# Two attention-then-MLP layers on one core: three positions in the hand-written step plan are changed

## The chip, the core and the metric

One core of a Trainium2 chip runs the whole program, built in Bass with every wait written by hand. The metric is device time in microseconds. The kernel before takes 3954.84 us, the median of three runs (3951.35 to 3958.53).

Five engines work side by side, each through its own queue of instructions in program order: TensorE (PE, matmuls into PSUM), VectorE (DVE), ScalarE (ACT), GpSimd (POOL), and SyncE (SP), which here only issues DMAs. An instruction that waits for a semaphore holds back all that stands behind it on its engine.

## What is computed

Input x is 4 sequences of 1024 tokens with 512 channels. Two transformer layers follow each other, each with 16 heads of width 32 and an MLP of width 2048. Cut to what matters:

```python
# layer 0
h = ada_norm(x, cond); q, k, v = h @ wq + bq, h @ wk + bk, h @ wv + bv
q, k = rotary(q), rotary(k)
x = x + softmax(q k^T / sqrt(32)) v @ wo + bo
x = x + gelu(ada_norm(x, cond) @ w1 + b1) @ w2 + b2
# layer 1: 4 key/value heads shared by 16 query heads, gates from the condition
h = ln(x) * (1 + sc1) + sh1
x = x + g1 * (softmax(q k^T / sqrt(32)) v @ wo.T)
x = x + g2 * (gelu((ln(x) * (1 + sc2) + sh2) @ w1.T + b1) @ w2.T + b2)
```

Products are made of two float16 halves of each operand (three matmuls for one), except values and totals, which are float32.

## The kernel before

The work is eight passes `i` = 0 to 7: layer 0 for the four sequences, then layer 1. Each pass is an attention and a forward part (the MLP). Both are written out by steps, and each engine's program walks the same steps.

**The attention** has 64 steps (`STEPS`), eight for each of eight blocks (4 heads by 512 queries). Step `s` computes four score tiles of 128 keys by 512 queries, `w` = 4s to 4s+3; two tiles make a unit `u`, so units 2s and 2s+1. Scores use three PSUM banks. ACT takes the exponential of each tile into `probs`, which has room for six units (L1209). PE multiplies the units of two steps before with the values (`values`, L1029). For the softmax's denominators POOL adds the probabilities of units u-2 and u into `sums`, which has three slots (`add_probs`, L730): sum 2p and 2p+1 need the units of step 2p+1. The last eight sums (56 to 63) of a pass are added by DVE (L1525). Then `totals` (L1044) multiplies the pair of sums 2p and 2p+1 with ones, on PE. `totals_step` says in which step PE does that for pair p; it stands at the end of the step, after the values.

Three waits tie these together. ACT writes unit u only when the sum that holds unit u-6 is done (L1204): units 4p+6 and 4p+8 wait for sum 2p, units 4p+7 and 4p+9 for sum 2p+1. The add of sum m waits for the totals of pair (m-3)//2 (L727, L1524). Totals wait for both sums of their pair (L1035).

**Beside it** PE computes the raw scores of the following block (`max_in_columns`, mostly four tiles per step, none in steps 56 to 63), and DVE takes each row's maximum (L1532); in the steps with s % 8 == 6, `max_rows` brings the maxima of a block together (DVE `mfin` L1537, a transpose on PE L977, `mT` on DVE L1541). These tiles, and all "fills", go through three more PSUM banks in turn. Fills are other products put between the scores of chosen steps (`fills_of`): projections of queries, keys and values; from step `WO_AT` the output products of the first half of the tokens, one per step (`out_tile`, keys `wo`), each read by DVE's `residual` (L1496 to L1505); in steps `LN2_AT` and `LN2_AT`+1 the second norm's chunks, two per step (`norm_chunk` on PE L852 and ACT L1167, `norm_lo` on DVE L1453, L1454). After the fourth output product DVE gathers the statistics (L1418, L1420), POOL computes the deviation (L708, L710) and DVE applies it (`norm_apply`, L1430) in its program order in that same step. DVE adds its sums at the end of a step, in steps 57 to 63 (`vector_step`).

**In layer 0** POOL also turns the queries and keys (`turns`: L715, L716, L720, L721) and adds a bias to eight tiles of x (L738, at the sums named in `BIAS_AT`, 49 to 56). In passes 0 to 3 ACT and DVE also split weights into halves for later (`SPLITS`: ACT L1235, DVE `split_low` L1582): each split takes two steps of DVE, from step 3 on in every third step, 18 splits in pass 0 and seven in passes 1 to 3. After each block ACT copies the outputs (L1215) and totals (L1221), POOL multiplies with the inverse (L762), and both finish the block (ACT L1191, in layer 0 also L1195; POOL L768), in fixed places: the values' copy in step 1 of the next block, the totals' copy in step 3, the finish of the block before that at the end of step 2.

**The forward part** has 33 steps of PE-heavy products. Its first product needs the second norm's chunks, and stands behind the last totals in PE's order.

Of the kernel before, what the change touches and what calls it, by code (L numbers as in the profile page):

```python
# [38 lines left out]
L0_CHUNKS, L1_CHUNKS = 24, 21  # L39
MAX_AT = (4, 6, 8, 10, 12, 14, 16, 18, 20, 22, 24, 26, 28, 30, 32)  # L40
MAX_AT_K = (0, 2, 5, 7, 9, 11, 14, 16, 18, 20, 23, 25, 27, 29, 32)
WO_AT = 53
LN2_AT = 60
BIAS_AT = (49, 49, 50, 51, 53, 54, 56, 56)
TURNS = ((("k", 1, 0), -1, 1, 5), (("k", 1, 1), 3, 3, 10), (("q", 0, 1), 11, 13, 29), (("q", 1, 1), 25, 27, 57))

# [1 line left out]
def layer(i):  # L48
    return i // B
# [30 lines left out]
def totals_step(i, pair):  # L80

    if pair >= SUMS // 2 - 2:
        return STEPS - 1 if pair == SUMS // 2 - 2 else STEPS + 1
    return 2 * pair + (3 if layer(i) == 0 and pair < 2 else 4)


def by_vector(m):
# [11 lines left out]
def fills_of(i):  # L99
# [12 lines left out]
    for t in range(4):  # L112
        at[WO_AT + t] = [("wo", i, t)]
    for t in range(2):
        at[LN2_AT + t] = [("ln2", i, 0, 2 * t), ("ln2", i, 0, 2 * t + 1)]
    return at
# [166 lines left out]
def program(nc, ins, out):  # L283
    ctx = ExitStack()
    with ctx:
# [546 lines left out]
        def _(pe):  # L832
# [215 lines left out]
            def attention(i):  # L1048
                for s in range(STEPS + LAG // 2):
                    u = 2 * s  # L1050
                    if s < STEPS:
                        maxima, fills = maxima_at(i, s), FILLS[i].get(s, [])
                        max_in_columns(maxima[0:1])
                        score(i, 4 * s)
                        max_in_columns(maxima[1:2])
                        score(i, 4 * s + 1)
                        for key in fills:
                            fill(key, 0, 6 if key[0] in "kqv" else 12)
                        max_in_columns(() if fills else maxima[2:3])
                        score(i, 4 * s + 2)  # L1060
                        for key in fills:
                            if key[0] in "kqv":
                                fill(key, 6, 12)
                        max_in_columns(maxima[2:3] if fills else maxima[3:4])
                        score(i, 4 * s + 3)
                        max_in_columns(maxima[3:] if fills else maxima[4:])
                    if LAG <= u < UNITS + LAG:
                        values(i, u - LAG)
                    for pair in range(SUMS // 2):
                        if s == totals_step(i, pair):  # L1070
                            totals(i, 2 * pair)
                    some(rows_at(i, s))
# [725 lines left out]
```

## Time and profile before

| | us |
|---|---|
| median of three runs | 3954.84 |
| lowest, highest | 3951.35, 3958.53 |
| the profiled execution, its time | 3957.61 |
| its span, first to last instruction | 3955.8 |
| busy: PE, DVE, POOL, ACT | 3746.3, 2471.2, 1613.5, 1603.8 |
| mean granted TensorE clock | 0.98 |

The rows below are of that one execution. Line numbers (L931) are those of the kernel before. A row of a timeline has the start, the duration, the engine, line and operation, what it writes and reads, how many instructions it joins, and, in brackets, how long the engine was idle before and what ended that. A matmul's duration is longer than its share of the engine, since matmuls overlap; what a group costs is read from one start to the next.

### The profile page before, as it was taken

To read this page: it belongs to the slowest core of one execution; us is meant where nothing else is said; L and a number is where in the kernel's file an instruction comes from. 1 tells how busy PE (TensorE), PEld (TensorE's weight loads), DVE (VectorE), ACT (ScalarE), POOL (GpSimd) and SP (SyncE) were. 2 spreads that over 40 slices of the span, in tenths; PEclk is the share of its full clock that TensorE was granted. 3 is DMA by queue.
4 is the path that set the end of the run, shared out by engine and by line. 5 is a ranking of instruction groups with operands and counts; after the bars stand their busy time and mean duration, and the time that the engine had idled before them with its cause. 6 is when DMAs were issued, how large, how long until landed. Compare 5 with 4: busy or idle time off the path is not lost.

```text
span 3955.8 us, 76367 instructions
## 1 busy us (share of the span) xinstructions
PE 3746.3 (95%) x31828; PEld 1559.4 (39%) x31828; DVE 2471.2 (62%) x3951; ACT 1603.8 (41%) x2807; POOL 1613.5 (41%) x907
## 2 busy tenths in 40 slices
PE   7988999999998989999899999999999999999999
PEld 4422444333543335433354333433344333543344
DVE  5677735766457755467654777467664776467752
ACT  1466313554125642155521663136621563126621
POOL 2467212672216742066510672137520672126611
PEclk8899999999999999999999999999999999999999
DMA  5233243212423123431232112311123112311122
GB/s 153 48 99 119 85 107 81 72 55 84 109 76 87 41 91 91 106 75 53 100 101 83 34 42 89 115 44 29 65 96 98 31 40 81 114 54 26 63 67 96
DMA packets 139110, 306.67 MB, mean 78 GB/s; under 512 B 19680, under 2 KB 59636, under 8 KB 137872
## 3 DMA queue, kind: packets, MB, share of 16 engines
q10 hardware_dynamic: 50944, 174.62, 13.6%
q1 hardware_dynamic: 87824, 127.17, 12.1%
q8 instruction: 253, 4.15, 0.4%
q14 instruction: 89, 0.73, 0.1%
HBM read 223.46 MB, written 36.66 MB: 66 GB/s over the span
## 4 chain that ended last, share of the span: by engine, by line
PE 79%; DVE 7%; POOL 5%; issue 4%; ACT 3%; DMA 1%; ACTq 0%; SPq 0%; POOLq 0%; DVEq 0%
PE ps L931 15%; PE ps L834 12%; PE ps L835 12%; PE ps L836 12%; PE ps L1029 9%; PE ps L871 7%; PE ps L1044 5%; PE ps L888 3%; POOL sums L730 3%; ACT probs L1209 3%; DVE mcol L1532 2%; PE ps L947 2%; PE ps L852 1%; DVE ring L1582 1%; DVE turn L1466 1%
## 5 line engine op out<-in xcount | busy, mean ns | idle before, releaser
L1532 DVE TENSOR_REDUCE mcol<-ps 128x1 f32<-128x512 f32 x2048 | 1290.0, 683 | 441.2 <-PE ps L931 226.7
L730 POOL TENSOR_TENSOR sums<-probs 128x1024 f32<-128x1024 f32 x448 | 1065.2, 2392 | 943.0 <-PE ps L1044 510.9
L1209 ACT ACTIVATE probs<-ps 128x512 f32<-128x512 f32 x2048 | 1098.8, 608 | 812.0 <-PE ps L931 564.3
L931 PE MATMUL ps<-qs,ks 98*32 98x512 f16 x8192 | 800.6, 389 | 105.4 <-ACT probs L1209 93.5
L931 PE MATMUL ps<-ks,qs 97*32 97x512 f16 x7040 | 697.3, 385 | 53.7 <-DVE mcol L1532 41.5
L1355 ACT ACTIVATE sums<-ps,cols 128x512 f32<-128x512 f32 x256 | 175.8, 687 | 1097.0 <-PE ps L836 1097.0
L1029 PE MATMUL ps<-probs,v_sb 128*32 128x512 f32 x4096 | 548.5, 612 | 0.0
L931 PEld LDWEIGHTS ps<-qs,ks 98*32 98x32 f16 x8192 | 215.5, 97 | 589.9 <-ACT probs L1209 363.9
L834 PE MATMUL ps<-ring,probs 128*128 128x512 f16 x1024 | 388.0, 379 | 0.3 <-DVE probs L1627 0.3
L834 PE MATMUL ps<-aT,ring 128*128 128x512 f16 x1024 | 388.1, 379 | 0.0
L836 PE MATMUL ps<-aT,ring 128*128 128x512 f16 x1024 | 388.0, 379 | 0.0
L835 PE MATMUL ps<-aT,ring 128*128 128x512 f16 x1024 | 387.9, 379 | 0.0
L836 PE MATMUL ps<-ring,probs 128*128 128x512 f16 x1024 | 387.9, 379 | 0.0
L835 PE MATMUL ps<-ring,probs 128*128 128x512 f16 x1024 | 387.8, 379 | 0.0
L931 PEld LDWEIGHTS ps<-ks,qs 97*32 97x32 f16 x7040 | 188.4, 96 | 375.8 <-DVE mcol L1532 150.5
L1626 DVE CAST probs<-sums 128x512 f16<-128x512 f32 x256 | 132.7, 518 | 320.2 <-ACT sums L1355 320.2
L871 PE MATMUL ps<-hT,wqkv 128*128 128x512 f16 x1248 | 302.7, 388 | 8.8 <-DVE hT L1454 7.5
L1044 PE MATMUL ps<-sums,ones 128*32 128x512 f32 x2048 | 276.2, 615 | 1.0 <-DVE sums L1525 1.0
L715 POOL TENSOR_TENSOR turn<-turn 128x512 f32<-128x512 f32 x32 | 44.9, 1403 | 532.5 <-DVE turn L1466 532.5
L1627 DVE TENSOR_TENSOR probs<-sums,probs 128x512 f16<-128x512 f32 x256 | 203.7, 796 | 8.8
L1466 DVE SCALAR_TENSOR_TENSOR turn<-ps,bias,trig 128x512 f32<-128x512 f32 x128 | 90.2, 747 | 167.1 <-PE ps L871 167.1
L871 PEld LDWEIGHTS ps<-hT,wqkv 128*128 128x128 f16 x1248 | 115.9, 99 | 172.6 <-issue 33.5
(112 smaller groups left out, 3471.9 us busy)
## 6 DMA issues: line engine op xcount, KB each, us to landing
ring<-halves ACTq DMA_DIRECT2D x208, 512.0 KB, 3.3
qs<-hl SPq DMA_DIRECT2D x192, 128.0 KB, 4.1
ring<-halves SPq DMA_DIRECT2D x48, 512.0 KB, 6.2
ring<-in_weights ACTq DMA_DIRECT2D x39, 512.0 KB, 4.6
halves<-ring ACTq DMA_DIRECT2D x37, 512.0 KB, 2.9
ks<-hl SPq DMA_DIRECT2D x120, 128.0 KB, 4.4
dcopy<-inverses SPq DMA_DIRECT2D x56, 256.0 KB
probs<-in_x SPq DMA_DIRECT2D x8, 1024.0 KB, 8.3
```

Source lines behind the costliest of these rows:

```text
L730: pool.tensor_tensor(sums[:, m % SUM_SLOTS, :, :], prob(u - 2), prob(u), ALU.add).then_inc(sum_set[0].sem, 1)
L834: pe.matmul(dst, lhs[0], rhs[0], start=first, stop=False)
L835: pe.matmul(dst, lhs[0], rhs[1], start=False, stop=False)
L836: return pe.matmul(dst, lhs[1], rhs[0], start=False, stop=last)
L871: mm = pe.matmul(bank, qkv(lw, weight_at(kind, i, hh, part, c), P), hT[:, lx, c, tok], start=(q == 0), stop=(q == 11))
L931: mm = pe.matmul(bank[cut, :], lhs[:, cut], rhs, start=True, stop=True)
L1029: mm = pe.matmul(ps[32 * q:32 * q + 32, 4, :], values_of(i, hh)[:, kt, value_cut(i, hh, 4 * g + q)], prob(u + q // 2)[:, q % 2, :], start= ...
L1044: mm = pe.matmul(ps[32 * q:32 * q + 32, 5, :], ones32[:, :], sums[:, (m + q // 2) % SUM_SLOTS, q % 2, :], start=(m % 8 == 0), stop=(m % 8 ...
L1209: act.activation(prob(u)[:, e, :], ps[:, w % SCORE_BANKS, :], ACT.Exp).then_inc(exp_done.sem, 1)
L1355: act.activation(g32[:, n % 2, :], ps[:, 4 + n % 2, :], ACT.Gelu, bias=col[:, n % FC:n % FC + 1], scale=1 / WS).then_inc(gelu_done.sem, 1)
L1532: dve.tensor_reduce(mcol[:, blk % 2, 4 * j + qt, half:half + 1], src, AX.X, ALU.max).then_inc(n_free[0], 1)
L1627: dve.tensor_tensor(fT[:, n % 4, 1, :], g32[:, n % 2, :], fT[:, n % 4, 0, :], ALU.subtract).then_inc(f_set.sem, 1)
```

## The change

`totals_step` gives step 2p+3 for every pair but the last two. Before, it gave 2p+4, except for the first two pairs in layer 0. `WO_AT` goes from 53 to 55: the output products of the first half of tokens are in steps 55 to 58. `LN2_AT` goes from 60 to 62: the second norm's chunks are in steps 62 and 63. `norm_apply` follows the fourth output product, so it moves to step 58 too. `BIAS_AT`, `vector_step`, and the places of all other work stay.

```diff
-WO_AT = 53
-LN2_AT = 60
+WO_AT = 55
+LN2_AT = 62
...
     if pair >= SUMS // 2 - 2:
         return STEPS - 1 if pair == SUMS // 2 - 2 else STEPS + 1
-    return 2 * pair + (3 if layer(i) == 0 and pair < 2 else 4)
+    return 2 * pair + 3
```

## Rows read from the trace of the kernel before

**Rows 1.** The page, part 1: busy us, share of the span, instructions.
```profile
PE 3746.3 (95%) x31828; PEld 1559.4 (39%) x31828; DVE 2471.2 (62%) x3951; ACT 1603.8 (41%) x2807; POOL 1613.5 (41%) x907
```

**Rows 2.** Waits: engine, line, waited for: us in total, times, longest.
```profile
PE ps L931 <- ACT probs L1209: 93.5, 135, 3.4
...
ACT probs L1209 <- POOL sums L730: 113.8, 84, 3.2
...
POOL sums L730 <- PE ps L1044: 510.9, 189, 8.9
```

**Rows 3.** Stretches: length, busy us of each engine, granted clock, DMA share, GB/s.
```profile
3138.84:3165.02 26.18, 25.64 (x357) 8.91 (x353) 20.78 (x35) 18.09 (x35) 21.17 (x10) 1.00 0.20 42
1235.62:1283.65 48.03, 39.54 (x490) 12.48 (x486) 40.51 (x59) 29.50 (x52) 37.91 (x18) 0.93 0.30 84
241.59:367.52 125.93, 108.23 (x1311) 35.49 (x1307) 103.16 (x150) 80.90 (x143) 85.27 (x42) 0.94 0.32 105
1283.65:1395.23 111.58, 108.03 (x1351) 38.98 (x1347) 79.46 (x133) 70.69 (x133) 80.32 (x43) 0.98 0.19 54
1395.23:1451.90 56.67, 47.05 (x433) 16.25 (x425) 30.62 (x44) 28.67 (x53) 25.85 (x17) 0.94 0.18 66
...
3262.43:3295.09 32.66, 28.74 (x249) 9.60 (x245) 18.51 (x32) 14.01 (x26) 15.34 (x9) 0.95 0.28 106
...
3295.09:3317.71 22.62, 19.04 (x188) 6.15 (x180) 14.63 (x16) 14.07 (x26) 1.60 (x1) 0.92 0.04 13
```

**Rows 4.** Timeline of PE, attention 6, steps 18 and 19.
```profile
3143.59 0.40 PE L931 MATMUL ps<-qs,ks 98*32 98x512 f16 x4 [0.36 <-ACT probs L1209]
...
3144.68 1.03 PE L1044 MATMUL ps<-sums,ones 128*32 128x512 f32 x8
3145.53 0.39 PE L931 MATMUL ps<-ks,qs 97*32 97x512 f16 x4
...
3148.14 0.39 PE L931 MATMUL ps<-ks,qs 97*32 97x512 f16 x4
```

**Rows 5.** Timelines of POOL and of ACT, attention 6, step 23.
```profile
3158.74 4.70 POOL L730 TENSOR_TENSOR sums<-probs 128x1024 f32<-128x1024 f32 x2 [1.70 <-PE ps L1044]
...
3161.23 2.06 ACT L1209 ACTIVATE probs<-ps 128x512 f32<-128x512 f32 x4 [0.78 <-POOL sums L730]
```

**Rows 6.** Timelines of DVE and of PE, attention 6, step 22.
```profile
3157.53 0.19 DVE L1537 TENSOR_REDUCE mfin<-mcol 128x16 f32<-128x32 f32 x1
...
3158.48 0.28 PE L977 MATMUL ps<-ident,mfin 128*16 128x128 f32 x1
```

**Rows 7.** Timeline of ACT, attention 2, end of step 34.
```profile
1327.07 0.77 ACT L1191 ACTIVATE aT<-ocopy,cols 128x512 f16<-128x512 f32 x1
```

**Rows 8.** Timeline of ACT, attention 2, end of step 17.
```profile
1255.35 1.08 ACT L1209 ACTIVATE probs<-ps 128x512 f32<-128x512 f32 x2 [2.92 <-POOL sums L730]
```

**Rows 9.** Timelines of DVE and of PE, attention 2, step 22.
```profile
1271.03 2.79 DVE L1582 SCALAR_TENSOR_TENSOR ring<-ring 128x512 f16<-128x512 f32 x1
...
1274.47 0.62 PE L931 MATMUL ps<-ks,qs 97*32 97x512 f16 x4 [1.88 <-DVE mcol L1532]
```

**Rows 10.** Timeline of PE, attention 6, step 55: first and last of twelve.
```profile
3277.11 0.39 PE L834 MATMUL ps<-wo,aT 128*128 128x512 f16 x1
...
3279.50 0.38 PE L836 MATMUL ps<-wo,aT 128*128 128x512 f16 x1
```

**Rows 11.** Timelines of POOL and of DVE, attention 2, step 58.
```profile
1423.19 1.02 POOL L710 TENSOR_TENSOR rs<-sd,eps 128x4 f32<-128x4 f32 x1
...
1424.25 2.77 DVE L1430 TENSOR_SCALAR v_sb<-ks,mv,rs 128x512 f32<-128x512 f32 x4 [6.63 <-POOL rs L710]
```

**Rows 12.** Timeline of DVE, attention 6, step 62.
```profile
3306.87 0.81 DVE L1453 TENSOR_SCALAR turn<-ps,ab 128x512 f32<-128x512 f32 x1 [1.49 <-ACT aT L1167]
...
3309.77 1.22 DVE L1525 TENSOR_TENSOR sums<-probs 128x1024 f32<-128x1024 f32 x1
```

**Rows 13.** Timeline of POOL, attention 2, step 51.
```profile
1391.28 2.52 POOL L738 TENSOR_TENSOR ks<-ks,row_bc 128x512 f32<-128x512 f32 x2
```

## The prediction

> **What bounds the kernel now.** I read first the page's busy times: TensorE (PE) works 3746.3 of 3955.8 us [rows 1]. So what can be won is the 209 us in which it stands, less the start, unless work is taken away, and this change takes none away. Second, the waits [rows 2]: PE waits 93.5 us for ACT's exponentials, ACT in turn 113.8 us in 84 places for POOL's sums, and POOL waits 510.9 us for PE's totals (L1044). That is a ring: totals release a slot of `sums`, POOL adds into it, the finished add releases a slot of `probs`, ACT writes it, PE may issue the next score. Third, stretches by stage [rows 3]: eight steps without fills in the second layer's blocks take 26.18 us; the layer 0 stretch of steps 13 to 23 takes 48.03 us at PE 39.54 busy; the last steps (from 53 to the first forward product) take 56.67 us in layer 0 and 32.66 + 22.62 = 55.28 in layer 1. Fourth, the timeline of single steps.
>
> A step without fills, in the shortest form that the trace has, runs from its first maximum to that of the next step in 2.61 us (3145.53 to 3148.14 [rows 4]). Totals add 0.86, from their start at 3144.68 to that maximum at 3145.53 [rows 4]: 3.47 us at best. The trace's even steps, which hold totals now, are longer than that. Attention 6, steps 16 to 23: 3.47, 2.61, 4.31, 2.61, 3.81, 2.61, 4.13, 2.61, the 26.18 of the stretch. In each odd step the third exponential waits for an add that could start only after the totals at the end of the step before: POOL starts two adds back to back, having waited 1.70 us for the totals [rows 5], and the exponential at 3161.23 waits 0.78 for the first of them [rows 5]. PE pays in the following even step: the score at 3143.59 waits 0.36 beyond its cadence [rows 4].
>
> **Part 1: totals in step 2p+3.** 30 of 32 pairs per attention move, save two in layer 0 that are there already and the last two. No instruction is added. The same 0.86 us of PE goes from an even to an odd step. The odd add of each pair waits for the pair before, now done one step earlier, so it starts as soon as its exponential is there: the adds (2.37 each [rows 5]) end well before the next odd step. Of eight steps: four odd ones at 3.47, three even at 2.61, and one with the rows of maxima. There the transpose (L977) follows the totals today, at 3158.48 [rows 6]. Without the totals in that step PE reaches it 0.86 earlier and waits until DVE's `mfin` is there (3157.53 + 0.19, in a step that now begins later by the stall above): it saves 0.6 of the 0.86, and that step takes 3.5. Sum 13.9 + 7.8 + 3.5 = 25.25, 0.93 less than 26.18. This is the cover that goes: totals hid a wait of DVE of about 0.6.
>
> A second cover goes. In every eight steps ACT ends step 2 with the finish of a block, two activations in layer 0 (0.77 us the first [rows 7], 1.4 for both). The totals hide that today. In a step of 2.61 the next exponential comes about 0.75 late and the fourth score with it, about 0.55: layer 0 gains 0.4 per eight steps, not 0.93. In layer 1 the single activation fits.
>
> Layer 1, steps 8 to 52: 5.6 times 0.93 = 5.2. Against it: step 14, where a fill's `hl` and two maxima follow the fill on DVE until `mfin`; that chain, not the totals, sets its end, so the moved 0.86 is simply added in step 13: minus 0.9. Steps 26 and 27 lose 0.6 in the same way (an estimate, from maxima 0.6 apart behind a fill). At the start POOL's first adds stand in line with four output sums, so totals in steps 3 and 5 wait for them on PE: minus 0.6. Net 3.1; ends 0 and 6.
>
> Layer 0, steps 13 to 23: here stalls are large. The exponential at 1255.35 waits 2.92 us for a sum [rows 8], and three before it 0.3 to 2.0, since POOL, with rotation and stack lows between its adds, starts each late. With one step more of slack these four go. And DVE's split (L1582) takes 2.79 us at 1271.03, where it starts 0.1 after an add and ends when that is over, and under 0.7 with POOL idle; PE then waits 1.88 for a maximum [rows 9]. **The rule**: the Trainium skill, SBUF — State Buffer, section "Who interferes with whom", says that a DVE instruction with two SBUF inputs and a GpSimd instruction that reads SBUF exclude each other for the whole of the one that came first. Here the row agrees. By that rule the change would move the blocks, not end them: see the third rival. From the rows: now adds start with the step in which the split is queued, so a blocked split waits for a whole add (2.1). After it, an add of an odd step starts at about 1.6 and ends at 4.0, the split comes at 2.6, so it waits 1.4; in an even step it waits 0.3. Stalls of PE in these eleven steps, counted as length less the cadence of every matmul group, are 14.8 us now; by the timeline drawn again with the same durations 8.5: 6 saved, ends 1 and 10.
>
> Layer 0, steps 24 to 52: POOL's second turning (steps 25 to 30) stalls 2.8 now and 0.6 then, minus 0.8 at step 26, plus 2.6 times 0.4: 2.4. In attention 0 these steps take 125.93 us against 111.58 in attention 2 [rows 3]; the difference is 22 more split halves and their blocks. By the same 1.4 and 0.3 half of them stay: another 5, ends 0 and 12. Steps 0 to 12: 0.5.
>
> **Part 2: output products at 55 to 58, second norm at 62 and 63.** A product is 12 matmuls, 3277.11 to 3279.50 and one more, 2.6 us [rows 10]. Of four, two leave steps 53 and 54, where DVE must also take maxima. They go to 57 and 58, which have neither fills nor maxima. Redrawn: steps 53 to 58 of layer 1 take 3.5, 3.35, 5.4, 4.5, 5.4, 4.5 = 26.7, with the same four products and three totals for which they take 32.66 now [rows 3]. What is late next is DVE's order. After the fourth product DVE does `ks`, stats and aggregates (1.9), POOL the deviation (1.3, of it L710 1.02), DVE four applications (2.77 [rows 11]; 1.9 with POOL idle) and only then the add of sum 57 (1.22 [rows 12]). Today that falls in step 56 and has two steps of room. At step 58 the add ends some 6.1 us into step 59 (5.3 in layer 0, which has one operation less per product). The exponential of unit 119 and the totals of pair 28 want it at 1.5 and 1.7: 4.4 us of stall, 3.6 in layer 0. Today steps 58 and 59 stall too, 4.3 in layer 1 and 6.7 in layer 0. At the end, chunks 3 and 4 now lie in front of the adds 62 and 63: from the add of 61, exponential, activation, two chunks of the norm (3306.87 to 3309.77, 2.9 [rows 12]), two adds and the totals in line make 0.6 + 0.8 + 2.9 + 2.5 + 1.0 = 7.8 us. Before them, from the start of step 62 to the end of the add of 61: 2.3 to the exponential behind the chunks' transposes, 1.4 to DVE, 2.9 for two chunks, 1.3: 7.9. Laid end to end, step 59 takes 7.2, 60 takes 2.2, 61 takes 2.9 and the rest 15.7: 28.0 us in layer 1, for 22.62 now [rows 3], and 27.1 in layer 0. Whole stretch: layer 1 54.7 against 55.28, 0.6 saved; layer 0 53.8. To that come 1.2, as POOL's bias additions (1.26 each [rows 13], with adds between them) make sum 51 late for totals now in step 53: 55.0 against 56.67, 1.7 saved. Ends for either: 4 lost, 6 saved. Nothing of this passes SP's or ACT's DMA queues: loads keep their places, and the reload of x, issued in step 49, had landed when these biases ran at 1391.28, two steps later [rows 13].
>
> **Sum.** Layer 1: 3.1 + 0.6 = 3.7, four times 15. Layer 0, attentions 1 to 3: 0.5 + 6 + 2.4 + 1.7 = 10.6, three times 32. Attention 0: 10.6 + 5 = 15.6, taken as 13, since its splits run on into steps 54 and 55. Together 60 us. The profiled execution took 3957.61 us with a span of 3955.8; the median shown is 3954.84. Profiled: 3957.6 - 60 = 3897.6; median 3954.8 - 60 = 3895.
>
> **Rivals.**
> 1. The mechanism holds as drawn: 3895. Chance 0.57.
> 2. PE waits for POOL. Totals a step earlier are in PE's program order, so whenever POOL is late the whole engine stands, where before only ACT did. For it: layer 0's rows of POOL, which is 37.91 of 48.03 us busy [rows 3]. Against it: an add ends 1.5 steps before its totals in the plain step. If it eats layer 0's gain but for the end, 15 + 7 remain: 3933. Chance 0.12.
> 3. The lock between DVE and POOL. If each of some 37 split halves in odd steps meets an add at its start (2.1 instead of 1.4, and 1.5 of it reaches PE), 0.7 to 1 more is lost for each: 30 us back, 3925. The same chance speaks for less: some pairs miss each other. This is what the Trainium skill's page SBUF — State Buffer would lead one to expect. Chance 0.13.
> 4. No change: the stalls of steps 58 to 63 double as the clock falls behind them (0.94 granted there, 1.00 in the plain steps [rows 3]), and the rest of the gain is eaten by them; 3950. The stalls are there today, so this needs 6 more per attention than drawn. Chance 0.08.
> 5. Slower: the end of attention. Add 57 behind the norm on DVE is a serial chain of five operations over two engines. Each of them late costs PE directly, and so do the adds 62 and 63 behind four chunks. If the two cost 4.4 + 8 us on top, not in place, of what stalls there now (12.4 in each of 8 attentions, 99 us) less 75 gained elsewhere, it is 24 slower: 3979. It decides from 7.5 us per attention on. Against it: today's stalls of 12 to 15 us in these steps have the same cause and go with it. Chance 0.10.
>
> Faster: 0.57 + 0.12 + 0.13 = 0.82; same 0.08; slower 0.10. 0.2%, 7.9 us, is about what a measurement of this kernel can tell from no change. Range: above, rivals 2 and 3 and the lower ends of layer 1 (0) and of the splits, 3938; below, the upper ends, some 30 us more, 3865.
>
> **What would show it.** ACT's wait for POOL's sums falls from 113.8 to under 40 us; POOL's wait for totals falls and its wait for ACT grows. Eight plain steps take 25.3 us, and L977 begins to wait for `mfin`, 0.5 each time. Split halves of 2.7 us become rare and halves of 2 common. A new wait of some 4 us stands in step 59, of PE for ACT and of ACT for DVE's sums. The prediction is wrong if PE waits for POOL's sums at L1044 for more than some 20 us in all, or if the last stretch is longer than 57 us.

## The result, and the profile after

The kernel after takes 3928.73 us (median; 3922.8 to 3928.93). Beside it, on the same chip, the kernel before took 3955.41 (3951.35 to 3958.53). The ratio is 0.993, with a 95% interval of 0.9912 to 0.9947: 26.7 us or 0.7% faster. Forecast were 3895 and a gain of 60. The direction and the range held, the size was over twice too large.

The page of the kernel after, span and busy times (us, share of the span, instructions), against [rows 1]:

```profile
span 3927.1 us, 76367 instructions
...
PE 3707.2 (94%) x31828; PEld 1609.8 (41%) x31828; DVE 2447.3 (62%) x3951; ACT 1609.2 (41%) x2807; POOL 1608.9 (41%) x907
```

The same 31828 matmuls take 39 us less of busy time, but the span is only 28.7 shorter. The waits of the kernel after (engine, what it works on, what it waited for: us in total, times, longest), against [rows 2]:

```profile
PE ps L1044 <- DVE sums L1525: 57.7, 24, 4.2
PE ps L977 <- DVE mfin L1537: 32.8, 54, 1.4
PE ps L931 <- ACT probs L1209: 20.8, 35, 1.3
...
PE ps L1044 <- POOL sums L730: 7.0, 9, 0.9
...
ACT probs L1209 <- DVE sums L1525: 48.5, 16, 4.5
ACT probs L1209 <- POOL sums L730: 18.1, 13, 2.0
...
POOL sums L730 <- PE ps L1044: 86.8, 46, 5.4
```

The old ring is open: ACT waits 18.1 us for POOL's sums (113.8 in [rows 2]), POOL 86.8 for totals (510.9), PE 20.8 for exponentials (93.5). At the top is a new wait: PE stands 57.7 us, in 24 places (three per attention), before totals whose sums **DVE** adds. These are the last sums of each attention.

I laid the step starts of the two traces beside each other. All eight attentions summed, in us:

| steps | after less before | forecast |
|---|---|---|
| 0 to 7 | +6.5 | |
| 8 to 12 | -14.3 | |
| 13 to 23 | -15.0 | |
| 24 to 52 | -30.1 | |
| 0 to 52 together | -52.9 | -50.4 |
| 53 to 58 | -27.0 | |
| 59 to 62 | -12.6 | |
| 63 to the first forward product | +57.9 | |
| 53 to the end together | +18.3 | -9.2 |
| forward parts (seven between attentions) | +5.7 | 0 |

The table tells of the two profiled executions, and that its row of steps 0 to 52 comes so near the forecast is in part luck (see below). Up to step 52 the sum is within 2.5 us of the forecast. Steps 53 to 62 gain 39.6, and the last stretch loses 57.9. That is where the expected gain went. The stretches that answer to [rows 3], of the kernel after (length, busy us of PE, PEld, DVE, ACT, POOL, granted clock, DMA share, GB/s): the plain eight steps of attention 6; steps 13 to 23 and 24 to 52 of attention 2; 24 to 52 of attention 0; then in attention 6 steps 53 to 58, 59 to 62, and from 63 on:

```profile
3110.99:3136.28 25.29, 24.78 (x357) 10.59 (x353) 20.63 (x35) 18.22 (x35) 21.28 (x11) 1.00 0.20 44
...
1218.12:1261.33 43.21, 36.46 (x499) 12.89 (x491) 38.99 (x61) 29.54 (x52) 33.45 (x17) 1.00 0.33 93
1261.33:1371.62 110.29, 106.98 (x1340) 42.75 (x1343) 77.72 (x131) 70.91 (x133) 82.58 (x43) 0.97 0.19 55
237.60:358.21 120.61, 103.12 (x1299) 36.19 (x1303) 105.08 (x149) 81.11 (x143) 90.69 (x45) 0.95 0.33 107
...
3233.58:3260.27 26.69, 26.18 (x251) 9.45 (x246) 15.37 (x24) 13.18 (x25) 11.39 (x6) 1.00 0.35 129
3260.27:3277.87 17.60, 12.60 (x124) 4.04 (x120) 9.26 (x16) 9.45 (x19) 3.62 (x4) 0.81 0.05 17
3277.87:3291.29 13.42, 8.08 (x68) 2.19 (x61) 9.23 (x11) 5.58 (x10) 0.00 (x0) 0.91 0.04 8
```

The plain block was forecast at 25.25 and takes 25.29. Steps 53 to 58 were forecast at 26.7 and take 26.69. The last two rows together are 31.02 us, for a forecast of 28.0, with PE standing over 10 of them.

**Step 59** of attention 6 in the kernel after. DVE's timeline, then POOL's, then PE's:

```profile
3263.09 2.74 DVE L1430 TENSOR_SCALAR v_sb<-ks,mv,rs 128x512 f32<-128x512 f32 x4 [1.41 <-POOL rs L710]
3265.76 2.35 DVE L1525 TENSOR_TENSOR sums<-probs 128x1024 f32<-128x1024 f32 x2
```
```profile
3262.04 1.02 POOL L710 TENSOR_TENSOR rs<-sd,eps 128x4 f32<-128x4 f32 x1
3263.03 1.15 POOL L768 TENSOR_TENSOR aT<-ocopy,aT 128x512 f16<-128x512 f32 x1
```
```profile
3267.07 1.94 PE L1044 MATMUL ps<-sums,ones 128*32 128x512 f32 x8 [4.16 <-DVE sums L1525]
```

DVE waits 1.41 us for the deviation, applies the norm in 2.74, and only then adds sums 57 and 58. PE waits 4.16 for the first of them. This is the stall that the forecast drew. Two of its sizes are not as drawn. The four applications take 2.74 and not 1.9, since POOL's finish of a block starts at 3263.03, 0.06 before them. And the eight matmuls of the totals take 1.94 us, where they take 1.03 in [rows 4].

### The profile page after: what moved, and what is told of

The parts are those of the page before. It is cut to its first block, busy times and chain, and to the rows that moved or that the text cites. A ratio compares the mean times of both kernels' runs of the same rounds, so it can differ in the third digit from the quotient of the medians.

```text
span 3927.1 us, 76367 instructions
## 1 busy us (share of the span) xinstructions
PE 3707.2 (94%) x31828; PEld 1609.8 (41%) x31828; DVE 2447.3 (62%) x3951; ACT 1609.2 (41%) x2807; POOL 1608.9 (41%) x907
## 4 chain that ended last, share of the span: by engine, by line
PE 80%; DVE 12%; issue 3%; POOL 2%; ACT 1%; DMA 1%; ACTq 0%; SPq 0%; POOLq 0%; DVEq 0%
PE ps L931 16%; PE ps L834 13%; PE ps L835 12%; PE ps L836 12%; PE ps L1029 8%; PE ps L871 7%; DVE mcol L1532 6%; PE ps L1044 5%; PE ps L888 3%; PE ps L947 2%; DVE ring L1582 1%; PE ps L852 1%; DVE sums L1525 1%; POOL sums L730 1%; ACT probs L1209 1%
## 5 line engine op out<-in xcount | busy, mean ns | idle before, releaser
L931 PE MATMUL ps<-qs,ks 98*32 98x512 f16 x8192 | 801.6, 388 | 26.6 <-ACT probs L1209 20.8
L931 PE MATMUL ps<-ks,qs 97*32 97x512 f16 x7040 | 708.2, 385 | 45.0 <-DVE mcol L1532 31.8
L931 PEld LDWEIGHTS ps<-qs,ks 98*32 98x32 f16 x8192 | 227.7, 98 | 357.5 <-ACT probs L1209 151.9
L931 PEld LDWEIGHTS ps<-ks,qs 97*32 97x32 f16 x7040 | 197.3, 96 | 407.1 <-DVE mcol L1532 206.5
L1044 PE MATMUL ps<-sums,ones 128*32 128x512 f32 x2048 | 280.1, 621 | 64.7 <-DVE sums L1525 57.7
```

The costliest lines, as they stand in the source:

```text
L931: mm = pe.matmul(bank[cut, :], lhs[:, cut], rhs, start=True, stop=True)
L1044: mm = pe.matmul(ps[32 * q:32 * q + 32, 5, :], ones32[:, :], sums[:, (m + q // 2) % SUM_SLOTS, q % 2, :], start=(m % 8 == 0), stop=(m % 8 ...
```

## The experiments

Each is compared with the kernel before on the same chip, whose medians lie from 3952.13 to 3957.19. "Tail" is step 53 to the first forward product, all eight attentions summed, less that of before. My theory: the two parts of the change (part 1, the totals' step; part 2, the places of products and chunks) are a gain and a cost, and the cost sits in DVE's order at the end of each attention.

### One part at a time

**Totals alone**, the kernel after with the other two positions as before:

```diff
-WO_AT = 55
-LN2_AT = 62
+WO_AT = 53
+LN2_AT = 60
```

> Totals in step 2p+3 as in the changed kernel, products and norm chunks left at 53 and 60. Theory A (the missing gain is in the last eleven steps, because the late products put DVE's norm in front of the add of sum 57): steps 0 to 52 keep their gain of some 53 us and the last stretch does not grow from 56 to 58 us per pass; total near 3900, at least 20 us under the changed kernel's 3928.7. Theory B (the two parts need each other: with products in steps 53 and 54 the totals of step 53 and the maxima stall, and moving them is what keeps the gain): 3930 or more.

Measured: 3869.02 us (3865.64 to 3873.46), ratio 0.9791 [0.9776, 0.9806]. That is 83 us off the kernel before, against 27 for the whole change, and below what either theory had said. Tail -27.6. Its waits, then from attention 6 its stretches of steps 53 to 58, 59 to 62, and from 63 on:

```profile
PE ps L931 <- ACT probs L1209: 41.4, 59, 1.7
...
PE ps L1044 <- DVE sums L1525: 9.7, 15, 0.9
```
```profile
3184.91:3215.49 30.58, 28.15 (x249) 9.74 (x245) 16.85 (x34) 13.01 (x25) 12.55 (x8) 0.94 0.30 113
3215.49:3230.99 15.50, 11.84 (x132) 4.49 (x128) 10.31 (x13) 11.89 (x23) 1.81 (x1) 1.00 0.05 18
3230.99:3238.37 7.38, 5.67 (x60) 1.50 (x53) 6.01 (x5) 3.09 (x6) 1.46 (x1) 1.00 0.02 6
```

PE's wait for DVE's sums is 9.7 us in place of 57.7. The tail of before was long because its totals were late, and earlier totals alone shorten it.

**Products and second norm alone**, the kernel before with `WO_AT = 55`, `LN2_AT = 62`:

> Products at 55 to 58 and chunks at 62 and 63, totals left as in the kernel before. Theory A: this part alone costs, some 2 to 4 us per pass in the last stretch: 3970 to 3985. Theory B: steps 53 and 54 lose their stall of some 2 to 3 us per pass and nothing comes in its place: 3930 to 3940.

Measured: 3975.42 us, ratio 1.0057 [1.004, 1.0074]: 23 us slower. Tail +11.9, forward parts +8.3. So part 1 alone brings 83 us, part 2 alone costs 23, and both bring 27: on top of part 1, part 2 costs 56. In the tail part 2 costs 11.9 us on top of the kernel before and 46.0 on top of part 1. The profiled executions of the kernel after and of totals alone lie 60 apart, 7.5 per attention. Of the 60, 46.0 are in the tail, 5.7 in the forward parts, and 7.5 in steps 0 to 52, most of it in attention 0 (last section).

**Products late, norm chunks early** (the kernel after with `LN2_AT = 60`):

> The changed kernel with the norm's chunks back in steps 60 and 61; the products stay late at 55 to 58. Theory A (each of the two moves costs by itself, in its own place): the stall of some 4 us at the totals of step 59 stays, the wait of the last totals behind two chunks and two adds goes; the last stretch is some 55 to 56 us instead of 57.8, total 3910 to 3920. Rival (the chunks do all the harm): some 52 us, total 3870 to 3880.

Measured: 3903.51 us, ratio 0.988 [0.9861, 0.9899]; tail +3.0, forward parts 0. That is a tail of 56 us per attention, as expected; the time is 6 us under the expected range.

**Products early, norm chunks late** (the kernel after with `WO_AT = 53`):

> The changed kernel with the products back at 53 to 56; the norm's chunks stay late in 62 and 63. Theory A: no stall at the totals of step 59, but from step 63 to the first forward product 13.4 us instead of 7.4, of which steps 60 and 61 give back 3 to 4; last stretch 54 to 56, total 3895 to 3915. Rival (the products do all the harm): 52 us, total 3870 to 3880.

Measured: 3894.15 us, ratio 0.985 [0.9833, 0.9867]; tail -17.1, forward parts +8.8. That is a tail of 53.5 us per attention, and it and the time are just under the expected ranges. Each half of part 2 costs by itself: in the tail, against -27.6, the products' move 30.6 and the norm's 10.5. Steps 59 to 62 of attention 6, and what follows, first products late with norm early, then the other way round:

```profile
3235.21:3256.63 21.42, 13.68 (x133) 5.14 (x128) 13.40 (x23) 11.93 (x23) 2.35 (x3) 0.92 0.04 13
3256.63:3264.01 7.38, 5.66 (x61) 1.50 (x54) 6.01 (x5) 3.09 (x6) 1.38 (x1) 1.00 0.02 7
```
```profile
3239.76:3251.25 11.49, 10.30 (x124) 3.63 (x120) 6.03 (x6) 9.44 (x19) 2.76 (x2) 1.00 0.08 26
3251.25:3263.81 12.56, 7.21 (x69) 2.15 (x61) 9.24 (x11) 5.57 (x10) 0.32 (x1) 1.00 0.01 2
```

The two costs have two places. With products late, PE stands in steps 59 to 62 (21.42 us at PE 13.68 busy). With chunks late, it stands from step 63 on (12.56 at 7.21).

### Only DVE's order changed

**Add 57 in front of the norm**, all positions as in the kernel after:

```diff
-                        if key == ("wo", i, 3):
-                            norm_apply("ln2", i, 0)
...
                             add_probs(i, m)
+                    if s == WO_AT + 3:
+                        norm_apply("ln2", i, 0)
```

> The changed kernel with one thing moved on DVE: in step 58 the add of sum 57 stands ahead of the four applications of the second norm, not behind them. Theory A: the stall of 4.2 us of PE at the totals of step 59 goes, step 59 falls from 8.5 to 4 us or less, eight passes give 30 to 40 us, 3890 to 3900. Rival: the applications, now 1.2 us later, or the clock, set the end all the same, 3920 to 3930.

Measured: 3894.4 us, ratio 0.9855 [0.984, 0.987]: 58 us off the kernel before, where the whole change takes off 27, with the same instructions. DVE's timeline of step 59 in attention 6, then the stretches of steps 59 to 62 and from 63 on:

```profile
3230.32 1.18 DVE L1525 TENSOR_TENSOR sums<-probs 128x1024 f32<-128x1024 f32 x1
...
3232.69 2.75 DVE L1430 TENSOR_SCALAR v_sb<-ks,mv,rs 128x512 f32<-128x512 f32 x4 [1.20 <-POOL rs L710]
```
```profile
3228.98:3242.15 13.17, 10.49 (x126) 3.70 (x121) 8.99 (x16) 9.56 (x19) 3.24 (x3) 1.00 0.06 19
3242.15:3255.84 13.69, 8.44 (x68) 2.71 (x61) 10.35 (x11) 5.56 (x10) 1.27 (x1) 0.87 0.02 6
```

The add no longer stands behind DVE's wait for POOL. Steps 59 to 62 fall from 17.60 to 13.17, all at the full clock, and the end stays as long. Against the kernel after, the tail is 29.3 us shorter; another 8.4 come in steps 0 to 52, most of them in attention 0, where no order was changed (last section).

**Adds 61 and 62 in front of the chunks too:**

```diff
                         max_item(key)
+                    if s >= 62:
+                        add_probs(i, s - 1)
...
-                        if by_vector(m) and vector_step(m) == s:
+                        if by_vector(m) and vector_step(m) == s and m not in (61, 62):
```

> As add57_first, and in steps 62 and 63 DVE adds sums 61 and 62 before the norm's chunks of the same step. Theory A: besides the stall of step 59, the exponential of unit 127 no longer waits 2.2 us for sum 61 and the last totals come one add earlier: another 2 to 4 us per pass, 3865 to 3880. Rival: the chunks, each later by an add, hold up the first forward product instead, as much as add57_first or more.

Measured: 3861.15 us, ratio 0.977 [0.9755, 0.9784]. Tail -39.0, forward parts +0.9. PE's waits, and steps 59 to 62 and from 63 on in attention 6:

```profile
PE ps L1044 <- DVE sums L1525: 15.0, 8, 2.2
```
```profile
3209.22:3224.03 14.81, 12.13 (x125) 3.95 (x120) 10.22 (x17) 9.56 (x19) 3.60 (x4) 0.88 0.06 20
3224.03:3233.90 9.87, 6.79 (x68) 2.18 (x61) 8.04 (x10) 5.56 (x10) 0.90 (x1) 1.00 0.01 2
```

The time is just under the expected range. The same matmuls at the same places now bring 91 us, 64 more than in the kernel after. So the cost of part 2 is DVE's order: instead of 56 us more than totals alone, the kernel takes 8 us less.

### The lock between DVE and POOL

Rival 3 said that DVE's splits would meet POOL's adds more dearly: each keeps the other out, as in [rows 9]. Here the low half of each weight split is written as zeros, so this part of the weights is left out, and the instruction reads nothing:

```diff
-                low = dve.scalar_tensor_tensor(out=pair[1][:, cut], in0=slot32[2 * (q % 3)][:, cut], scalar=split_scale(ch),
-                                               in1=pair[0][:, cut], op0=ALU.mult, op1=ALU.subtract)
+                low = dve.memset(pair[1][:, cut], 0.0)
```

In the kernel after:

> The changed kernel with DVE's split of the weights' low halves replaced by a write of zeros with no input from SBUF (so all low halves of the weights after the first ones are left out). Theory of the lock: in passes 0 to 3 the steps 13 to 52 lose the stalls that follow a blocked split, 8 to 12 us in pass 0 and 5 to 8 in each of 1 to 3; total 3928.7 less 25 to 35, so some 3895 to 3903. Rival (POOL's place in the ring, not the lock, sets these steps): under 10 us less.

Measured: 3896.24 us, ratio 0.9853 [0.9839, 0.9868]. In the kernel before:

> The kernel before with the same left out. Theory of the lock: it frees more here than in the changed kernel, since blocked splits of 2.7 us are more common: 40 to 50 us, 3905 to 3915, so the gain of the totals' step in layer 0 shrinks by 10 to 20 us when the splits are gone. Rival (the totals' step gains the same with or without the lock): the same difference to before as the other kernel has to the changed one, within 5 us.

Measured: 3908.66 us, ratio 0.9888 [0.9873, 0.9902]. Both came where the theory of the lock expected them; its rival, the same gain with and without splits within 5 us, is out. Without the splits the whole change is worth 12.4 us (3908.66 to 3896.24), with them 26.7. In steps 13 to 52 of layer 0 the splits cost 40.6 us before (657.9 with, 617.3 without) and 33.2 after (627.4, 594.3). So the lock was not made dearer, and 7.4 of the 30.4 us gained there go with the splits. The other 23.0 come with no splits at all, from totals a step earlier. What the splits cost is not all waiting: the write of zeros takes 0.27 us, for 0.62 to 0.69 of a split that meets nothing. In the traces with splits, those of over 2.4 us fall from 18 to 1 and those of 1.7 to 2.4 rise from 3 to 15, of 78, as the prediction had said. Waits of the kernel before without splits, and of the kernel after without them:

```profile
PE ps L931 <- ACT probs L1209: 87.5, 131, 3.4
```
```profile
PE ps L1044 <- DVE sums L1525: 57.7, 24, 4.2
```

Neither the old ring (93.5 in [rows 2]) nor the new stall (57.7 with splits too) is the splits' doing.

### A version that beats both

If DVE's order at the end is what counts, the kernel with totals alone should also gain: there, in steps 60 and 61, DVE's adds 59 and 60 stand behind chunks. **Adds first, `WO_AT` 53, `LN2_AT` 60:**

```diff
-WO_AT = 55
-LN2_AT = 62
+WO_AT = 53
+LN2_AT = 60
...
+                    if s in (LN2_AT, LN2_AT + 1):
+                        add_probs(i, s - 1)
...
-                        if by_vector(m) and vector_step(m) == s:
+                        if by_vector(m) and vector_step(m) == s and m + 1 not in (LN2_AT, LN2_AT + 1):
```

> Totals in step 2p+3, products at 53 and chunks at 60 as before, and in steps 60 and 61 DVE adds sums 59 and 60 before the chunks of the same step. Theory A (what costs in the last steps is work put in front of an add on DVE): the exponential of step 61 no longer waits 2.6 us for sum 59; 2 to 4 us less per pass than with the totals moved alone (3869): 3840 to 3855. Rival: the chunks end later by two adds and take it back, 3865 to 3875.

Measured: 3851.21 us, ratio 0.974 [0.9725, 0.9755]; tail -50.5. ACT's timeline at the end of step 61 in attention 6, first of totals alone, then of this kernel:

```profile
3226.95 0.60 ACT L1209 ACTIVATE probs<-ps 128x512 f32<-128x512 f32 x1 [2.63 <-DVE sums L1525]
```
```profile
3210.81 0.60 ACT L1209 ACTIVATE probs<-ps 128x512 f32<-128x512 f32 x1 [0.69 <-PE ps L931]
```

The wait of 2.63 us for DVE's sum is gone. **The same with `WO_AT` 54:**

> The same with the products at 54 to 57, so one fewer of them beside the maxima. Theory A: steps 53 to 55 lose one of the two stalls of some 2 us that the maxima and products make together, while the norm ends in step 58 and puts the add of sum 56 or 57 off by about 2 us: within 8 us of the kernel with products at 53, 3835 to 3860. Rival (a product later always costs): 3870 or more.

Measured: 3873.04 us, ratio 0.98 [0.9774, 0.9825]. This missed my expectation, and by its number the rival (a product later always costs) was right. DVE's timeline at the end of step 58 in attention 6 names another cause, and ACT's behind it:

```profile
3218.22 2.75 DVE L1430 TENSOR_SCALAR v_sb<-ks,mv,rs 128x512 f32<-128x512 f32 x4 [1.41 <-POOL rs L710]
3220.89 2.35 DVE L1525 TENSOR_TENSOR sums<-probs 128x1024 f32<-128x1024 f32 x2
```
```profile
3222.22 0.60 ACT L1209 ACTIVATE probs<-ps 128x512 f32<-128x512 f32 x1 [2.86 <-DVE sums L1525]
```

With the norm in step 57, add 56 stands behind it. I had looked at add 57 alone. **The norm behind these adds**, at the end of step 58:

```diff
-                        if key == ("wo", i, 3):
-                            norm_apply("ln2", i, 0)
...
+                    if s == WO_AT + 4:
+                        norm_apply("ln2", i, 0)
```

> As wo54_ln60_first (3873), but DVE applies the norm at the end of step 58, behind the adds of sums 56 and 57. Theory A (that kernel lost its 20 us to the wait of 2.9 for sum 56, which stood behind the norm): that wait goes and the kernel comes to 3840 to 3855. Rival (a product more beside or behind the maxima, or the clock, costs it): 3865 to 3875.

Measured: 3853.23 us (3849.46 to 3860.5), ratio 0.9738 [0.9723, 0.9752]: 104 us off the kernel before in place of 82, with the products at the same places. So it was the order, and not the product's place. **And in the best version**, `WO_AT` 53 with the norm at the end of step 57:

> As wo53_ln60_first (3851), but the norm is applied at the end of step 57, behind the add of sum 56. Theory A says little is left to win: that add had room, so within 6 us of 3851. Rival (the norm's place matters even where no wait is seen): 3840 or less, or 3860 or more if the chunks of step 60 come to wait for it.

Measured: 3850.52 us, ratio 0.9723 [0.9707, 0.974], not to be told from 3851.21. With products at 53 the norm stands ahead of add 56 by one step more, and was out of its way already. These versions are 2.6 to 2.8% faster than the kernel before and about 2% faster than the kernel after.

## Why the prediction was right and where it was wrong

**Part 1, right, and nearly to size.** In layer 1 the odd and even steps, the step with maxima and the plain block came as drawn, and L977 does wait for `mfin`: 32.8 us in 54 places, 0.6 each. Steps 0 to 52: layer 1 was forecast at -3.1 per attention and gave -4.5 in the mean; layer 0's attentions 1 to 3 at -8.9 and gave -8.6; attention 0 at -11.3 and gave -9.0. That the sum agrees within 2.5 us is in part luck: layer 1 gained 5.6 us more than drawn, and attention 0 lost some 6 to a single split (by its length with totals alone, last section). The stalls of steps 13 to 23 in attention 2 fell from 14.8 to 9.1, for a forecast of 8.5. The length there fell by only 4.8, as the eleven steps now hold one more totals (0.86), which the forecast overlooked; the following stretch has it back. In steps 24 to 52, attentions 1 to 3 gave 6.1, 1.3 and 1.8 for a forecast of 2.4 each: 9.2 in sum for 7.2, and not right in each.

**The end of attention, wrong.** It was forecast at -9.2 us and came at +18.3, a miss of 27.5. Two things make it up, and a third stands behind it.

First, the term of step 59 and of the end was too small. Layer 1 takes 57.8 for 54.7, layer 0 58.1 for 55.0, so 3 us are missing in each attention, 25 in all. In attention 6, step 59 takes 8.47 for 7.2, step 60 3.23 for 2.2, and the rest 19.32 for 18.6. The two steps in the kernel after:

```profile
3260.27:3268.74 8.47, 3.75 (x36) 0.90 (x32) 6.81 (x14) 3.38 (x7) 2.35 (x3) 0.77 0.01 3
3268.74:3271.97 3.23, 3.23 (x30) 0.90 (x24) 1.22 (x1) 2.07 (x4) 0.00 (x0) 0.54 0.03 6
```

Step 60 has no stall at all: PE is busy for 3.23 of 3.23 us. Its granted clock is 0.54, so most of it ran at the lower of the two levels (1.2 GHz), behind PE's wait of 4.16. The forecast priced the stall and not the slower matmuls behind it: 0.8 in the totals of step 59 (1.67 from their start to the next step, for 0.86 in [rows 4]), 1.0 in step 60, and 0.9 in the last totals, which show the same in PE's timeline:

```profile
3282.68 1.06 PE L1044 MATMUL ps<-sums,ones 128*32 128x512 f32 x8 [0.55 <-DVE sums L1525]
...
3289.43 1.93 PE L1044 MATMUL ps<-sums,ones 128*32 128x512 f32 x8 [3.23 <-DVE sums L1525]
```

After a wait of 0.55 they take 1.06, after one of 3.23 they take 1.93. The length of the last wait alone does not decide it: in the kernel before, behind the wait of 1.88 in [rows 9], eight matmuls of the values took as long, where they take 1.03 elsewhere, and the clock granted from 1274.47 to 1277.20 was 0.50:

```profile
1275.30 1.93 PE L1029 MATMUL ps<-probs,v_sb 128*32 128x512 f32 x8
```

Rival 4 had named the falling clock, but asked for six more us per attention and gave it 0.08. What it named came at under four of those six: the 3 here, of which 0.5 is not the clock's, and 0.8 in each forward part.

The rest of step 59's miss, 0.5, is the add of sum 57, which ends later, since the norm takes 0.8 longer. The cause is the first application of the norm beside POOL's finish of a block: it takes 1.37 us, the other three 0.54 each (one begins before the last has ended). With totals alone nothing of POOL stands beside the norm, and the four take 1.92:

```profile
3213.10 1.92 DVE L1430 TENSOR_SCALAR v_sb<-ks,mv,rs 128x512 f32<-128x512 f32 x4 [1.41 <-POOL rs L710]
```

The same 2.77 stood in [rows 11], and I had taken 1.9 "with POOL idle" without asking whether POOL would be idle. The Trainium skill, SBUF — State Buffer, section "Who interferes with whom", lists `tensor_scalar` among the operations that can hold the pair of ports shared with GpSimd; the rows of step 59 agree, with 0.06 us between the two starts.

Second, 2.6 us are the base: I compared with the 55.28 of attention 6 in [rows 3], while the four of layer 1 take 54.6 in the mean.

Third, the forward parts. They were forecast at 0, and took 5.7 us more, which the 27.5 does not hold. In the six kernels here with the chunks in steps 60 and 61 they took 0.0 more. With chunks at 62 and 63 they took 5.7 to 8.8 more, and 0.9 when the adds stand in front of the chunks, where the last wait of PE is 2.04 us in place of 3.23 and its totals take 1.06. The stretch of the kernel after from the last totals into the first forward products:

```profile
3288.80:3292.20 3.40, 2.77 (x11) 0.59 (x12) 0.48 (x1) 0.77 (x2) 0.00 (x0) 0.50 0.39 117
```

The granted clock is 0.50 here, and the forward part starts in it.

**The step of the reasoning that failed** is larger than these sizes. Against rival 5 the prediction said that today's stalls in the tail "have the same cause and go with it", with "it" the whole change. The runs show that they go with part 1 alone: its tail is 27.6 us shorter. Part 2 then brings in stalls of its own, 46 us in the tail. The redrawn tail held both parts at once and was compared with before, where late totals hid most of the same DVE chain. It never was drawn with part 1 alone, so the price of part 2, 7.5 us per attention, stood nowhere in the sum. Rival 5's mechanism, add 57 and the last adds queued behind the norm and the chunks, is the one that the runs confirm. It did not turn the sign, since part 1 alone gains 83 us and part 2 takes back 56 of them. Rival 5's threshold of 7.5 us per attention does not follow from its own terms: against the 75 us that it grants elsewhere it is 75 / 8 = 9.4, and 7.5 is 60 / 8, where 60 already holds the end's saving.

**The other rivals.** Rival 1, the mechanism as drawn, fails at the end of attention and holds before it. PE does not wait for POOL: 7.0 us in all, under the 20 set as the mark. The lock did not get dearer: 33.2 us for 40.6. The second mark, a last stretch over 57 us, was passed, at 57.8 and 58.1.

## What to carry to other kernels

Price each part of a change on top of the others, not only the sum against before: a stall of before can hide a chain that one part lengthens and another uncovers. When a step is moved, read the in-order queue of each engine that it uses and list what stands behind its waits; here, moving a few adds to the front was worth 64 us with no work changed. To a long wait of PE add the slower matmuls behind it, here 1.7 to 1.8 us for each wait of 3.2 to 4.2.

## What the runs showed that I had not expected

**One split waits for four instructions of POOL, not one.** DVE's splits into `ring`, 74 of the 78 (shortest, median and longest in ns; first and last start), in the kernel before and in the kernel after:

```profile
L1582 DVE SCALAR_TENSOR_TENSOR ring<-ring x74: 616/693/2794, 175.9 to 1789.5; 128x512 f16<-128x512 f32 x74
```
```profile
L1582 DVE SCALAR_TENSOR_TENSOR ring<-ring x74: 616/757/7443, 174.5 to 1765.0; 128x512 f16<-128x512 f32 x74
```

The one of 7.44 us stands in attention 0, step 52. DVE's timeline and POOL's beside it, in the kernel after:

```profile
347.15 7.44 DVE L1582 SCALAR_TENSOR_TENSOR ring<-ring 128x512 f16<-128x512 f32 x1 [0.99 <-ACT ring L1235]
```
```profile
346.92 2.39 POOL L730 TENSOR_TENSOR sums<-probs 128x1024 f32<-128x1024 f32 x1
349.25 1.28 POOL L738 TENSOR_TENSOR ks<-ks,row_bc 128x512 f32<-128x512 f32 x1
350.47 2.36 POOL L730 TENSOR_TENSOR sums<-probs 128x1024 f32<-128x1024 f32 x1
352.76 1.28 POOL L738 TENSOR_TENSOR ks<-ks,row_bc 128x512 f32<-128x512 f32 x1
```

The split starts 0.23 us after an add, and ends 0.55 after the fourth instruction of an unbroken row on POOL (352.76 + 1.28 = 354.04). It does not get its turn between them, and PE waits 6.6 us for the maxima behind it. The Trainium skill, SBUF — State Buffer, section "Who interferes with whom", calls the shared pair of ports an exclusive lock, and says of DVE's two-port modes that whoever issues first gets it "for the whole instruction". This row, of a DVE instruction with two SBUF inputs, shows the loser kept out for four. The wait of 6.6 us is in the traces of five of the kernels (after, both adds first, products at 53 with chunks at 62, and the two with the norm later). In totals alone, where PE's longest wait for a maximum is 2.3, steps 24 to 52 of attention 0 take 6.3 us less than in the kernel after. So some 6 us of a difference between two kernels here can be this one split and not the change. What decides whether the split falls into such a row was not tried. The times of one kernel lie some 6 us apart in places (3922.8 beside three of 3928.6 to 3928.9 for the kernel after), which would fit, but no profile of a shorter run was taken.
